# A scan and feed-forward layer on eight cores: ScalarE's token-tile work set a step behind VectorE's, decay tiles and casts moved to GpSimd, stream tiles moved out of the scan

## What is computed

```
z    = x Wi^T ; gate = silu(x Wg^T)                    # 128 scan channels
dt   = softplus(z Wdt^T + b_dt)
s_k[t] = (1 - dt[t] exp(A_log[:,k])) s_k[t-1] + dt[t] z[t] B_k[t]   # 16 states k
y    = (sum_k C_k s_k) * gate ; a = y Wo^T
x1   = layernorm(x + a)
h    = x1 * rsqrt(mean(x1^2) + eps) * w_norm
q    = round(127 h / max|h|) per token
gv   = q . ternary(w_gv), with scale mean|w_gv|         # 2 x 8192 rows
u    = value * silu(gate)
out  = layernorm(x1 + quant(u) . ternary(w_out))
```

## Time and profile before

| | |
|---|---|
| profiled execution, own time | 3115.05 us |
| its span, slowest core | 3113.4 us (cores 3090.8 to 3113.4) |
| runs: lowest, median, highest | 3122.33, 3147.95, 3298.08 us |
| busy: TensorE, VectorE, ScalarE, GpSimd | 87%, 63%, 53%, 15% |
| DMA | 645.28 MB, mean 207 GB/s |
| chain that ended last | PE 60%, DVE 15%, DMA 9%, issue 8%, ACT 7% |
| GB/s in the first eight of 40 slices | 316 325 316 280 285 306 295 193 |

### The profile page before, as it was taken

One profiled execution on the slowest core, in us unless ns is written; L12 is line 12 of the kernel. 1 busy time (PEld: TensorE's weight loads), 2 busy tenths in 40 slices (PEclk: granted clock), 3 DMA queues, 4 the chain that ended last, 5 costly groups with the idle time before them and its releaser, 6 DMA issues.

```text
span 3113.4 us, 36732 instructions; the slowest of 8 cores (3090.8 to 3113.4 us)
## 1 busy us (share of the span) xinstructions
PE 2708.0 (87%) x12080; PEld 1203.1 (39%) x12080; DVE 1954.3 (63%) x2027; ACT 1648.0 (53%) x1996; POOL 466.7 (15%) x305
## 2 busy tenths in 40 slices
PE   3354541399999999999999999999999999999998
PEld 1111210144444444444444444444444444444443
DVE  3688786678777787777778777776462342332421
ACT  3675864466767667768888888887110100100000
POOL 0000000223222222222323223221000000000000
PEclk8666665699999999999999999999999999999999
DMA  9998888567777777767788888876963242332420
GB/s 316 325 316 280 285 306 295 193 192 220 213 222 219 214 216 218 226 196 231 233 236 230 241 227 244 231 233 211 309 195 116 82 163 81 115 129 81 152 71 27
DMA packets 264524, 645.28 MB, mean 207 GB/s; under 512 B 17872, under 2 KB 165376, under 8 KB 239120
## 3 DMA queue, kind: packets, MB, share of 16 engines
q1 hardware_dynamic: 172944, 522.77, 55.5%
q10 hardware_dynamic: 86016, 83.90, 7.7%
q0 software_dynamic: 5376, 36.27, 3.5%
HBM read 540.63 MB, written 102.24 MB: 206 GB/s over the span
## 4 chain that ended last, share of the span: by engine, by line
PE 60%; DVE 15%; DMA 9%; issue 8%; ACT 7%; ACTq 1%; DVEq 0%; POOL 0%; SPq 0%; POOLq 0%
PE pvg L830 30%; PE pvg L1049 28%; DVE wop L735 4%; DMA ringb<-wgvt 4%; DMA ring<-wgvt 3%; ACT ring L764 3%; DVE sg L865 1%; DVE ub L870 1%; DVE res L451 1%; DVE sg L878 1%; DVE stk L357 1%; ACT sn L845 1%; DVE accg L266 1%; DMA ring<-xq 1%; ACT ringb L254 1%
## 5 line engine op out<-in xcount | busy, mean ns | idle before, releaser
L830 PE MATMUL pvg<-q,wop 128*128 128x512 f16 x4096 | 952.0, 380 | 7.3 <-ACT wop L725 3.5
L721 POOL TENSOR_SCALAR ring<-ring,wsc 128x1024 f32<-128x1024 f32 x254 | 437.9, 1727 | 1168.7 <-DMA ring<-wgvt 1096.1
L830 PEld LDWEIGHTS pvg<-q,wop 128*128 128x128 fp8e4 x4096 | 401.2, 98 | 497.9 <-issue 22.2
L845 ACT COPY sn<-pvg 128x512 f32<-128x512 f32 x512 | 294.5, 581 | 309.7 <-PE pvg L830 248.1
L1049 PE MATMUL pvg<-qob,Tb 128*128 128x512 fp8e4 x2048 | 444.6, 379 | 0.0
L1069 ACT ACTIVATE pvg<-Ta 128x2048 f32<-128x2048 f32 x16 | 30.1, 1882 | 775.9 <-DVE Ta L1065 775.9
L830 PE MATMUL pvg<-Ta,wop 128*128 128x512 f16 x1536 | 364.5, 380 | 15.1 <-ACT sn L845 11.1
L830 PE MATMUL pvg<-Tb,wop 128*128 128x512 f16 x1536 | 364.5, 380 | 1.2 <-ACT sn L845 1.2
L1065 DVE SCALAR_TENSOR_TENSOR Ta<-pvg,c2c,Ta 128x2048 f32<-128x2048 f32 x16 | 37.6, 2350 | 467.5 <-PE pvg L1049 467.5
L1049 PEld LDWEIGHTS pvg<-qob,Tb 128*128 128x128 bf16 x2048 | 200.6, 98 | 241.8 <-issue 0.6
L865 DVE TENSOR_TENSOR sg<-pvg,sn 128x1024 f32<-128x1024 f32 x128 | 156.8, 1225 | 174.6 <-PE pvg L830 118.5
(11 more groups left out here) (167 smaller groups left out, 2822.0 us busy)
## 6 DMA issues: line engine op xcount, KB each, us to landing
ring<-woutT SPq DMA_DIRECT2D x256, 512.0 KB, 5.4
ring<-wgvt SPq DMA_DIRECT2D x252, 512.0 KB, 6.5
ringb<-wgvt SPq DMA_DIRECT2D x77, 1024.0 KB, 11.9
u_sp<-ub ACTq DMA_DIRECT2D x128, 512.0 KB, 4.2
ring<-u_sp SPq DMA_DIRECT2D x128, 512.0 KB, 5.2
ring<-wgvt SPq DMA_DIRECT2D x51, 1024.0 KB, 12.2
res<-xn POOLq DMA_DIRECT2D x16, 1024.0 KB, 11.3
qo_sp<-qo_t ACTq DMA_DIRECT2D x128, 128.0 KB, 6.3
```

The costliest lines, as they stand in the source:

```text
L721: t = eng.do(lambda e: e.tensor_scalar(out=ap, in0=ap, scalar1=wsc[:, 1:2], scalar2=MAGIC, op0=ALU.mult, op1=ALU.add))
L830: t_pr[(n, name)] = pe.do(lambda e, k=k, w=w, m=m, o=o, first=first: e.matmul(o, w[:, k * 128:(k + 1) * 128], m[:, k * TS:(k + 1) * TS], s ...
L845: t_sn[(n, name)] = ac.do(lambda e: e.copy(out=sn[:, i * TS:(i + 1) * TS], in_=bank(h, b)))
```

## The change

- `emit_ak` is on GpSimd (a multiply-add) with a buffer of three tiles; `xq_cast` is on GpSimd for quarters 1 to 3.
- `abs_dve` is gone from steps 0 to 63 and from the first 8 steps behind them; from t = 72 on it takes one tile a step. The loop is three steps longer, and the rest of the tiles is taken beside the rows of scales.
- ScalarE's square goes into a buffer of its own, and stands one step later; `mean` and `stats` are apart; the roots stand at the start of the step after the statistics, ahead of that step's stream tile; ScalarE's rounding, the input load (now on ScalarE's list), and the transposes stand one to two steps later. In each step ScalarE's stream tile now comes ahead of its token-tile work.
- `bsums` is spread, one difference in every second step from t = 67 on, and that of the second half beside the rows of scales, with `Tb` placed once the front's left buffers are given back.
- In set n = 0 value halves are ternarized one by one between the products.

```diff
-    def cast_in(src, out):
+    def cast_in(src, out, eng=dv):
...
-        t_cast[(q, c)] = cast_in(xq[q, c], o)
+        t_cast[(q, c)] = cast_in(xq[q, c], o, po if q else dv)
...
-        ac.wait(t_na[0], t_dt[q], t_st.get(t - 2))
-        t_ak[t] = ac.do(lambda e: e.activation(out=half(ak, t), in_=half(dt_s, q),
-                                               func=AF.Identity, scale=nega[:, k:k + 1],
-                                               bias=1.0))
+        po.wait(t_na[0], t_dt[q], t_st.get(t - 3))
+        t_ak[t] = po.do(lambda e: e.tensor_scalar(out=akb(t), in0=half(dt_s, q),
+                                                  scalar1=nega[:, k:k + 1], scalar2=1.0,
+                                                  op0=ALU.mult, op1=ALU.add))
...
-            po.wait(t_qb.get(i - NX))
-            t_xn[i] = po.dma(xslot[i % NX], lambda e: e.dma_start(out=rs(i), in_=xn[i]))
+            ac.wait(t_qb.get(i - NX))
+            t_xn[i] = ac.dma(xslot[i % NX], lambda e: e.dma_start(out=rs(i), in_=xn[i]))
...
-        ac.wait(t_s1[(i, 0)], t_s1[(i, 1)], t_tr.get((i - 2, 1)), t_qb.get(i - 2))
-        t_sq[i] = ac.do(lambda e: e.activation(out=qbi(i), in_=rs(i), func=AF.Square,
+        ac.wait(t_s1[(i, 0)], t_s1[(i, 1)], t_sq.get(i - 1))
+        t_sq[i] = ac.do(lambda e: e.activation(out=sqj[:], in_=rs(i), func=AF.Square,
...
@@ tiles(t), steps of a pair; t >= 16
             elif s == 1:
                 add_res(a, 1)
                 wo_mm(b, 0)
-                square(a)
             elif s == 2:
+                square(a)
                 add_res(b, 0)
                 wo_mm(b, 1)
             elif s == 3:
                 add_res(b, 1)
+                mean(a)
+            elif s == 4:
                 square(b)
-            elif s == 4:
-                stats(a)
                 g_of(a)
             elif s == 5:
-                stats2(a)
+                stats(a)
                 g_of(b)
             elif s == 6:
+                stats2(a)
+            elif s == 7:
                 scales(a)
                 round_dve(a)
...
+        if t >= 24 and (t - 24) % 8 < 6 and (t - 24) // 8 < NT // 2:
+            g, s = divmod(t - 24, 8)
+            a, b = 2 * g, 2 * g + 1
+            order = [(a, 0), (a, 1), (b, 0), (b, 1)]
+            if s == 0:
                 round_act(a)
                 xload(a + NX)
-                trans(a, 0)
-            elif s == 7:
                 round_dve(b)
+            elif s == 1:
                 round_act(b)
                 xload(b + NX)
...
+                trans(a, 0)
             else:
-                trans_out(b, 1)
+                trans_out(*order[s - 2])
+                if s < 5:
+                    trans(*order[s - 1])
...
@@ the loop over t
-    for t in range(NSTEP + 16 + 3):
+    for t in range(NSTEP + 16 + 6):
...
+        if t + 2 < NSTEP:
+            emit_ak(t + 2)
+        roots(t)
+        abs_act(2 if t < NSTEP and t % 4 == 3 else 1)
         tiles(t)
...
-            abs_act(2 if t % 4 == 3 else 1)
-            if t % 4 == 1:
-                abs_dve(1)
-        else:
-            abs_act(1)
+        elif t >= NSTEP + 8:
             abs_dve(1)
-        if t == NSTEP + 4:
-            dv.wait((ac.h, ac.n), (pe.h, pe.n), (dv.h, dv.n), t_ysp[3])
+        if t == NSTEP + 3:
+            dv.wait(t_ak[NSTEP - 1], t_y[NSTEP - 1], t_pc[NSTEP - 1], t_ysp[3], (dv.h, dv.n))
...
+        if tsum and t % 2 == 0:
+            next(tsum, None)
...
@@ for b in range(NTS): rows of scales
         abs_dve(1)
+        next(tsum, None)
...
-    abs_act(200)
+    for _ in range(2 * HC):
+        abs_act(1)
+        abs_dve(1)
     abs_dve(2, keep=True)
...
@@ the entry
     wsums(0, GATE)
-    for i in range(4):
-        tern_half(0, VAL, i)
...
+        if n == 0:
+            tern_half(0, VAL, 0)
+            products(n, [2])
+            tern_half(0, VAL, 2)
...
             products(n, [1])
             snap(n, "p7")
+            tern_half(0, VAL, 1)
             products(n, [3])
...
+        if n == 0:
+            tern_half(0, VAL, 3)
+            t_mx0 = po.do(lambda e: e.memset(Mx[:], 0.0))
+            wsums(0, VAL)
```

More of the change, by code:

```diff
@@ L231, in build_program @@
     t_car = dv.do(lambda e: e.memset(carry[:], 0.0))
-    def cast_in(src, out):
+    def cast_in(src, out, eng=dv):
         s, ap, tok = ring_load(src)
-        dv.wait(tok)
-        t = dv.do(lambda e: e.tensor_copy(out=out, in_=ap))
+        eng.wait(tok)
+        t = eng.do(lambda e: e.tensor_copy(out=out, in_=ap))
         rfree[s].append(t)
@@ L357, in scan_dve @@
         t_st[t] = dv.do(lambda e: e.tensor_tensor_scan(
-            out=half(stk, t), data0=half(ak, t), data1=half(uk, t),
+            out=half(stk, t), data0=akb(t), data1=half(uk, t),
             initial=carry[:, k:k + 1], op0=ALU.mult, op1=ALU.add))
@@ L421, in square, with root, mean @@
     def square(i):
-        ac.wait(t_s1[(i, 0)], t_s1[(i, 1)], t_tr.get((i - 2, 1)), t_qb.get(i - 2))
-        t_sq[i] = ac.do(lambda e: e.activation(out=qbi(i), in_=rs(i), func=AF.Square,
+        ac.wait(t_s1[(i, 0)], t_s1[(i, 1)], t_sq.get(i - 1))
+        t_sq[i] = ac.do(lambda e: e.activation(out=sqj[:], in_=rs(i), func=AF.Square,
                                                accum_out=col(SSQ, i)))
-    def root(i0, dst, src):
+    def root(i0, k, dst, src):
+        c = lambda kind: col(kind, i0, 2)
+        ac.wait(t_stat[(i0, k)], t_eps)
+        t_rt[(i0, k)] = ac.do(lambda e: e.activation(out=c(dst), in_=c(src), func=AF.Sqrt,
+                                                     bias=epsc[:]))
+    def mean(i0):
         c = lambda k: col(k, i0, 2)
-        ac.wait((dv.h, dv.n), t_eps)
-        return ac.do(lambda e: e.activation(out=c(dst), in_=c(src), func=AF.Sqrt, bias=epsc[:]))
+        dv.wait(t_s1[(i0 + 1, 1)])
+        chain(lambda e: e.tensor_add(out=c(SUM), in0=c(SUM), in1=c(SUMB)),
+              lambda e: e.tensor_scalar_mul(out=c(MU), in0=c(SUM), scalar1=1.0 / D),
+              lambda e: e.tensor_mul(out=c(MU2), in0=c(MU), in1=c(MU)))
     def stats(i0):
@@ L433, in stats @@
         dv.wait(t_sq[i0], t_sq[i0 + 1])
[L434 to L439, removed]
+        t_stat[(i0, 0)] = dv.do(lambda e: e.scalar_tensor_tensor(
+            out=c(VAR), in0=c(SSQ), scalar=1.0 / D, in1=c(MU2), op0=ALU.mult, op1=ALU.subtract))
     def stats2(i0):
@@ L443, in stats2 @@
         dv.wait(t_rt[(i0, 0)])
-        chain(lambda e: e.reciprocal(out=c(RS), in_=c(SD)),
-              lambda e: e.tensor_mul(out=c(V1), in0=c(VAR), in1=c(RS)),
-              lambda e: e.tensor_mul(out=c(V2), in0=c(V1), in1=c(RS)))
-        t_rt[(i0, 1)] = root(i0, SD2, V2)
+        t_stat[(i0, 1)] = chain(
+            lambda e: e.reciprocal(out=c(RS), in_=c(SD)),
+            lambda e: e.tensor_mul(out=c(V1), in0=c(VAR), in1=c(RS)),
+            lambda e: e.tensor_mul(out=c(V2), in0=c(V1), in1=c(RS)))
     def g_of(i):
-        dv.wait(t_wn)
+        dv.wait(t_wn, t_sq[i])
         t_g[i] = dv.do(lambda e: e.scalar_tensor_tensor(
@@ L559, in bsums, with bops @@
         dv.wait(t_T[(p, 2)])
+        yield
         t_T[(p, 4)] = sub(T4, B(1, 0), T2)
+    def bops(p, T):
+        B = lambda kh, q: q1[:, ((2 * p + q) * DC + 8 * kh) * TS:
+                             ((2 * p + q) * DC + 8 * kh + 8) * TS]
+        T1, T2, T3 = (T[:, i * 8 * TS:(i + 1) * 8 * TS] for i in range(3))
+        T4 = B(0, 1)
         return {"B11": B(0, 0), "B21": B(1, 0), "B22": B(1, 1), "T1": T1, "T2": T2, "T3": T3,
@@ L1117, in build_program @@
             combine(n - 1, 1)
-        if s == 0:
+        if s == 0 and n:
             wsums(jp, VAL)
```

62 lines of the change are left out of this document (34 added, 28 removed).

## The result

The changed kernel ran at 3069.72 us in the median of four runs (3068.76 to 3126.52); its ratio to the kernel before is **0.9836, interval 0.9804 to 0.9868**. Runs in which one die was disturbed are left out of the ratios. The profiled execution took 3068.76 us with a span of 3067.2, where before it was 3115.05 and 3113.4: 46 us less. Forecast were 40 less, 3075, or 3082 with the offset.

What follows compares the result with a forecast made beforehand. VectorE and the DMA were taken to run neck and neck in the scan, holding each other up in turn. First product 32 us earlier and entry 8 give -40 on 3115, 3075; plus 7, 3082 us, range 3040 to 3130.

Steps and rivals of the forecast that it cites:

- The 7 us that I added for the runs: Added to the sum of 3075 because the profiled execution was 7 us below the fastest run shown, giving 3082 us.
- The end: Between last landing and first product: one reduction and 4.5 us remain, 6.8 us where 27.7 were.
- The entry: Start of the feed-forward part: of TensorE's 10.0 us waiting for ScalarE's copies 2 remain, -8 us.
- The landing: Last weight tile lands at 560 us, not 571, with the scan ending at 405, not 463.
- ScalarE a step behind: Token tiles: later squares and split statistics shorten no large wait between VectorE and ScalarE; counted at nothing.
- the missing waits at VectorE's own tiles: Scan: without VectorE's 7% of waiting at its own stream tiles, the larger sum over the length rises from 0.88 to 0.94.
- The new wait: Scan: the input load, issued two steps later, makes VectorE wait 2 us a pair, 4 a stretch; ends 0 and 20.
- It costs no more than before: Scan: a GpSimd decay tile waiting behind a cast costs nothing extra, as VectorE did that waiting itself before.
- The slower rival: Steps 16 to 63: all 60 us of GpSimd's work come onto VectorE, +24 us, 3146; chance 0.10.
- a third of it: Partial rival: a third of GpSimd's 60 us comes onto VectorE, scan ends 21 us later, 3103; chance 0.18.
- The full-DMA rival: Front: DMA share 0.97 up to the landing, first product at 539 us, -68 us, 3054; chance 0.27.

Runs made afterwards that it cites:

- u_entry: The changed kernel with set 0 of the feed-forward part in the old order, all value ternaries ahead of the first copy; ratio 0.9841 to the kernel before.
- b_stream: The kernel before with only VectorE's stream tiles moved out of steps 0 to 71 to behind the scan; ratio 0.9975 to the kernel before.
- sched: The changed kernel with VectorE's stream tiles back in the scan, casts back on VectorE and decay tiles on ScalarE; ratio 0.9904 to the kernel before.
- v_early: The changed kernel with ScalarE's rounding of a pair's first tile and the input load ahead of that step's stream tile; ratio 0.9802 to the kernel before.
- u_akcast: The changed kernel with decay tiles back on ScalarE and all casts back on VectorE; ratio 0.9823 to the kernel before.
- v_both: The changed kernel with v_early's earlier rounding and input load, and each decay tile ahead of the same step's cast on GpSimd; ratio 0.9805 to the kernel before.
- v_more: v_both with four more ScalarE stream tiles in the last 16 scan steps and four fewer behind the scan; ratio 0.9813 to the kernel before.
- v_light: v_both with a token tile's largest value taken over 128 of 2048 elements, giving wrong scales; ratio 0.9804 to the kernel before.

## Why the prediction was right and wrong

**The size.** -40 us of 3115 were forecast, a ratio of 0.987; measured were 0.9836 and 0.9853, 51 and 46 us. The change is plain in the measurement, and a change within 2% was called likeliest, which is where it lies, though near its edge. The 7 us that I added for the runs lay the other way: the profiled execution's time was already below all three runs shown, and the time of the changed kernel (3069.72) lies under even the sum without them.

**The end, as forecast.** One reduction and 4.5 us between the last landing and the first product: 6.8 forecast, 6.8 measured. Bringing the rows, transposes and differences beside the stream did what it says; this is 21 of the 43 us at the slowest core's first product.

**The entry: as forecast in its gaps, not at the end.** 8 us forecast; TensorE's gaps fell from 7.7 to 10.1 over the cores to 0.9 to 2.9. Half of it is the order of set 0, half the early differences (u_entry). The forecast had no term for the granted clock, which rose from 0.80 to 0.83 over the cores in the 34 us behind the first product to 0.91 to 0.96; with both, the lead is 12 us after 100 us. It cost all that follows at nothing, and there half of the lead or more is lost again: 6 us are left at the median, 3 between the slowest cores. So the 40 of the forecast came as 43 + 3 there, not as 32 + 8.

**The landing: nearly the right result, by the wrong step.** Forecast 560, measured 549 (scan 405 and 401, the tail 155 and 148 us). That these are close is luck. The step that failed is the one that I counted at nothing: *ScalarE a step behind*. "Neither engine's wait for the other is among the large ones" was read from VectorE's waits alone. ScalarE's list had 59 us of them, and ScalarE is the engine that empties most of the ring. The forecast's own rows had it too: the earlier trace rows give 74.7 us of idle time ahead of L474, put down to L469. In its place I gave the rise of the share to the missing waits at VectorE's own tiles ("without the 7% of waiting at its own tiles I take 0.94"). b_stream has those waits taken away and the share stays at 0.85 to 0.89; sched has them all in place and the share is 1.00. Such a wait costs VectorE its time, but it did not empty the DMA (share full in the longest of them): the tile that is waited for is on its way, the others behind it too.

The two parts need each other for the time. At the median core's first product, the schedule alone gives 16 us (sched), the stream tiles alone 5 (b_stream), together 36. The difference of 15 us is well over the 6 between two executions. Alone, the schedule finishes loads in the scan that are then missing as cover behind it (share 0.79), and the moved tiles find a scan in which ScalarE still stands in long waits (share 0.85).

**The new wait, right in place and too small.** 2 us a pair were forecast for the input tile; 25.6 us over the six pairs of these stretches were measured, 4.3 a pair. The load lands in 14.0 us in place of 11.3, which I put down to the fuller DMA; no run separates that from the later issue. v_early, which issues it sooner, starts the first product 5 to 11 us sooner. The sum hid it, because the DMA's share came out higher than 0.94 in the second and third stretch (0.95 and 0.98) all the same; in the fourth it was 0.88.

**GpSimd.** Forecast 0.75 and 3.0 us for a decay tile and a cast, measured 0.83 and 2.0. "It costs no more than before" was right in the time (u_akcast, v_both against v_early), though VectorE does wait 19.4 us in four for a decay tile over the front. The slower rival, all of GpSimd's time on VectorE, did not show, nor a third of it: the scan instruction takes 1.320 us in the mean, 1.277 before, 2.8 us in 64. The mean hides how: nine of the 64 took 1.47 to 1.67 us, each beside a cast or a decay tile on GpSimd. With GpSimd's part undone (u_akcast) the mean is 1.279.
The Trainium skill (SBUF — State Buffer, Who interferes with whom) has it that a VectorE instruction with two SBUF inputs contends with a GpSimd one that reads SBUF. The trace agrees: the scan has its inputs in SBUF, and each of the nine long ones ran beside a GpSimd instruction that reads SBUF. Of the 64 decay tiles 33 waited for a scan's end, and those run in the main beside the two products that read PSUM, whose means did not move (0.68 and 0.66 us).

**The full-DMA rival** (share 0.97, first product at 539) was the nearer one for the share (115.4 + 95.5 + 90.7 + 78.3 + 145.0 = 525 us of full share in 549, 0.96), but 525 and not 516: the same 174 MB go at 332 GB/s of full share in place of 338, and in v_both, with a share of 0.98 over the front, at 327. So the last idle stretches of the DMA are worth less than their length. Why a full share carries less is open; it was not tried. From there on the front is close to bound by its loads: v_more and v_light moved work and tiles and left the ratio where it was.

## What to carry to other kernels

Where a ring of loads is emptied by two engines, read the waits of the engine that empties most of it, and ask at each whether landed tiles lie behind it: a wait for a tile was harmless to the stream, a wait for the other engine drained it where it lasted 7 to 10 us, and much less in pieces of 4 to 6. Look at the longest waits, then, and not at their sum. Hand work between two in-order engines over a step late, so that the taker seldom stands long; and when that fills the DMA early, move loads to where the work will be, or the tail has no cover. Delaying a step delays its buffer's release too: the load that hangs on it has to be followed to its reader.

## What the runs showed of the hardware

- A cast of 128x2048 from f32 to bf16 took 1.89 us on GpSimd where nothing held it and 1.23 on VectorE; 128x512 f32 through TENSOR_SCALAR took 0.69 us on GpSimd in the median, with a longest of 2.80.
- In stretches of 50 us with a DMA share of 0.96 to 1.00 a core was given 295 to 349 GB/s (all cores, all runs), with eight at it. Over the front a full share was worth 338 GB/s in the kernel before (share 0.90), 332 in the changed one (0.96) and 327 in v_both (0.98). In the kernel before, the cores were 20 us apart at the first product (580.6 to 600.7), and in the changed kernel 2 us in one execution and 18 in another.
- The Trainium skill (HBM Reference, Specifications (TRN2)) gives some 358 GB/s for each of two cores that share a memory domain; nothing here came above 349 in such a stretch.
